# Causal attention on one core: row-score jobs in two PSUM banks, column-score jobs in four

## The reference, cut to what matters

```
dot  = einsum('bqhd,bkhd->bhqk', q, k)              # q, k scaled
dot  = where(tril, dot, -inf)
attn = softmax(dot, axis=-1)
out  = einsum('bhqk,bkhd->bqhd', attn, v) @ Wo
```

## Time and profile before

| | us |
|---|---|
| median of three timed runs | 4139.68 (4137.76 to 4142.01) |
| the profiled execution's own time | 4147.65 |
| its span in the profile | 4145.7 |
| PE busy in the span | 3816.1 |
| DVE busy | 2304.2 |
| ACT busy | 1747.5 |

### The profile page before, as it was taken

How to read it: one execution, slowest core, us unless ns; L and a number is a source line. 1 busy time by engine, 2 the same in 40 slices (tenths; PEclk the granted TensorE clock), 3 DMA queues, 4 the chain that set the end, 5 groups by cost and what they waited for, 6 DMA issues and landing times.

```text
span 4145.7 us, 77057 instructions
## 1 busy us (share of the span) xinstructions
PE 3816.1 (92%) x30311; PEld 2466.6 (59%) x30431; DVE 2304.2 (56%) x7434; ACT 1747.5 (42%) x3560; POOL 813.5 (20%) x1373
## 2 busy tenths in 40 slices
PE   7999999988899999998899989999889998999988
PEld 3555567665455556766545546676654555666665
DVE  4545444677454545467654554546765454454776
ACT  3324333466332433346633242335663334233566
POOL 3102013321110202332011020233302102023330
PEclk9999999999999999999999999999999999999999
DMA  2000000000000000000000000000000000000000
GB/s 81 1 1 1 1 1 1 2 2 1 12 1 1 1 1 1 1 2 2 5 8 1 1 1 1 1 1 2 2 6 7 1 1 1 1 1 1 2 2 6
DMA packets 19694, 17.06 MB, mean 4 GB/s; under 512 B 2604, under 2 KB 18941, under 8 KB 19325
## 3 DMA queue, kind: packets, MB, share of 16 engines
q1 hardware_dynamic: 19325, 11.99, 1.0%
HBM read 9.89 MB, written 2.10 MB: 3 GB/s over the span
## 4 chain that ended last, share of the span: by engine, by line
PE 70%; DVE 11%; ACT 8%; POOL 7%; issue 4%; DVEq 0%; POOLq 0%; SPq 0%
PE banks L1033 8%; PE banks L1047 8%; PE banks L1043 8%; PE banks L926 6%; PE banks L958 5%; POOL work L507 4%; PE banks L970 3%; PE banks L911 3%; PE banks L1142 3%; PE banks L1277 2%; ACT work L783 2%; PE banks L831 2%; ACT work L777 2%; PE banks L1114 2%; PE banks L1087 2%
## 5 line engine op out<-in xcount | busy, mean ns | idle before, releaser
L1454 DVE CUSTOM_DVE_ANT_0 work<-banks,mask_row 128x512 f32<-128x512 f32 (+3 forms) x1024 | 444.2, 487 | 248.3 <-PE banks L926 246.3
L669 ACT ACTIVATE work<-banks 128x384 f32<-128x384 f32 (+1 forms) x768 | 357.6, 532 | 373.9 <-PE banks L958 372.2
L687 ACT ACTIVATE work<-banks 128x512 f32<-128x512 f32 (+1 forms) x384 | 227.7, 596 | 650.7 <-PE banks L1043 641.8
L926 PE MATMUL banks<-work 32*128 32x512 f32 (+3 forms) x2048 | 421.5, 460 | 13.0 <-ACT work L662 13.0
L958 PE MATMUL banks<-work 32*128 32x512 f32 (+3 forms) x2048 | 425.8, 464 | 4.3 <-DVE work L1463 4.3
L474 POOL TENSOR_SCALAR_AFFINE_SELECT work<-work 128x128 f32<-128x128 f32 (+1 forms) x768 | 250.1, 332 | 878.8 <-ACT work L669 860.5
L1531 DVE TENSOR_TENSOR work<-work,banks 128x512 f32<-128x512 f32 (+1 forms) x384 | 261.1, 686 | 280.2 <-PE banks L1047 280.2
L464 POOL TENSOR_TENSOR rstd<-rstd,half 128x4 f32<-128x4 f32 x64 | 64.6, 1009 | 1755.2 <-DVE rstd L1388 1755.2
L1033 PEld LDWEIGHTS banks<-wd,work 128*128 128x128 f32 (+1 forms) x3072 | 359.3, 191 | 49.1 <-issue 49.1
L1033 PE MATMUL banks<-wd,work 128*128 128x128 f32 (+1 forms) x3072 | 361.1, 274 | 0.0
L926 PEld LDWEIGHTS banks<-work 32*128 32x128 f32 x2048 | 232.4, 183 | 167.1 <-DVE work L1454 93.6
(11 more groups left out here) (312 smaller groups left out, 6723.0 us busy)
## 6 DMA issues: line engine op xcount, KB each, us to landing
wg<-in_L_ffn_Wg_dram SPq DMA_DIRECT2D x1, 1376.0 KB
wu<-in_L_ffn_Wu_dram SPq DMA_DIRECT2D x1, 1376.0 KB
x_a<-in_L_attn_a_x_dram SPq DMA_DIRECT2D x4, 256.0 KB, 2.8
x_b<-in_L_attn_a_x_dram SPq DMA_DIRECT2D x4, 256.0 KB, 2.9
wd<-in_L_ffn_Wd_dram SPq DMA_DIRECT2D x2, 512.0 KB
out_dram<-x_a SPq DMA_DIRECT2D x4, 256.0 KB, 2.3
out_dram<-x_b SPq DMA_DIRECT2D x4, 256.0 KB, 2.5
wk_l<-in_L_attn_a_Wk_dram SPq DMA_DIRECT2D x1, 512.0 KB, 6.2
```

The lines of the kernel that those rows point to most:

```text
L669: eng.activation(prob4[:, G % 2, hh, C_AT[j]:C_AT[j] + C_N[j]], bank(column_bank(c))[:, 0:C_N[j]], ACT.Exp).then_inc(s_exp, 1)
L926: m = eng.matmul(bank(k % 3)[:, col:col + N], q4[own, G, P * t:P * t + P], k4[own, G, 0:N], start=True, stop=True)
L1454: m = eng.tensor_tensor_reduce(out=summed[:, k % 2, col:col + N], in0=bank(k % 3)[:, col:col + N], in1=mask_row[:, T - N:T], scale=1.0, sc ...
```

## The change

Row jobs turn in two banks (0 and 1) in place of three, so row job k waits for the maximum of job k - 2. Column jobs up to 32 turn in four banks (2 to 5) in place of three and wait for the exponential of the job four before. From job 33 on the five banks come in the order 1, 3, 4, 5, 2, and only job 33 still waits for all row maxima; job 34 waits for an exponential as the later ones do.

```diff
         def column_bank(c):
-            return 3 + c % 3 if c < WIDE else 1 + (c - WIDE) % 5
+            return 2 + c % 4 if c < WIDE else (1, 3, 4, 5, 2)[(c - WIDE) % 5]
...
             def score_rows(k):
...
-                if k >= 3:
-                    eng.wait_ge(s_max, JOBS4 * n + k - 2)
+                if k >= 2:
+                    eng.wait_ge(s_max, JOBS4 * n + k - 1)
...
-                    m = eng.matmul(bank(k % 3)[:, col:col + N], q4[own, G, P * t:P * t + P], k4[own, G, 0:N],
+                    m = eng.matmul(bank(k % 2)[:, col:col + N], q4[own, G, P * t:P * t + P], k4[own, G, 0:N],
...
             def score_columns(c):
...
-                if WIDE <= c < WIDE + 2:
+                if c == WIDE:
                     eng.wait_ge(s_max, JOBS4 * (n + 1))
-                elif c >= WIDE + 2:
+                elif c > WIDE:
                     eng.wait_ge(s_exp, JOBS4 * n + c - 4)
-                elif c >= 3:
-                    eng.wait_ge(s_exp, JOBS4 * n + c - 2)
+                elif c >= 4:
+                    eng.wait_ge(s_exp, JOBS4 * n + c - 3)
...
                 def row_max(k):
...
-                        m = eng.tensor_tensor_reduce(out=summed[:, k % 2, col:col + N], in0=bank(k % 3)[:, col:col + N],
+                        m = eng.tensor_tensor_reduce(out=summed[:, k % 2, col:col + N], in0=bank(k % 2)[:, col:col + N],
```

## The result

The changed kernel takes 4573.11 us (median of four runs, 4562.64 to 4575.5) against 4140.62 us before: a ratio of 1.1044, 95% interval 1.1026 to 1.1063. It is slower by 432 us, 209 more than forecast, and above the upper end of the range, 4440.

The account below looks back on a forecast made before the run. PE, busy 92% and 70% of the chain, was taken as the bound, with row jobs waiting for the vector engine. Bank turns summed to 13.96 us a call, times 16 = 223 us, giving 4363 us; range 4250 to 4440.

Parts of the forecast that it names:

- the early part: From a call's first row job to the values, four bursts of three row jobs: +6.73 us a call.
- the middle part: From the values to the first column job: +0.62 us a call.
- the joint part: From the first column job to the weighing behind row job 47: +1.83, +1.26, +0.50, +0.48 twice, +1.03 twice, us a call.
- points 3 to 6: Jobs 16 to 23 +1.83; 24 to 26 +1.26, 36 to 38 +0.50; two fours +0.48 each; two fives +1.03 each.
- Points 1 and 3 to 6: First: projecting part's four bursts, third job waits for the first, +1.92, +1.61, +1.56, +1.64 us; the others: job groups from 16 on.
- Point 7: Fourth bank of the column jobs: gains at most 1.7 us a call, at least nothing; taken as nothing.
- the third rival: PE's granted clock falls to half through the projecting part: 159 us on top, 4522 us; 8%.
- The joint part hides nothing: Answers the rival that from k = 16 on existing waits hide the new ones: only 118 us, 4257 us; 12%.
- The not-slower case: PE's own stream is the bound, and the fourth column bank gives back 26.8 us: 4113 us; 5%.
- the signs that I named: Row waits doubled, 200 to 300 us; column waits near nothing; bursts 2.4 to 3.0 us; first column job 7.4 later; clock 1.00.

Follow-up runs that it names:

- the kernel with the fill before row job 14: Changed kernel plus idle products before each early burst's third job and one before row job 14, none in the joint part; 4444.22 us.
- the moved third job: Changed kernel with the third row job of each early burst put behind the next projection, the last burst's behind the values; 4433.9 us.

## Why the prediction was wrong, and what of it was right

**The sum was right, its clock was not.** At full clock the early part grew by 16.30 - 9.53 = 6.77 us (forecast 6.73), the middle part by 5.51 - 4.92 = 0.59 (0.62), the joint part by 34.52 - 27.92 = 6.60 (points 3 to 6: 1.83 + 1.26 + 0.50 + 0.96 + 2.06 = 6.61). That is 13.96 us a call, 223 us in all, and the kernel that fills the stops comes to 4378 us. Points 1 and 3 to 6 hold one by one too. The bursts of an early part at full clock without idle products (call 10 of the kernel with two banks there alone) grew by 2.00, 1.58, 1.55 and 1.63 us (forecast 1.92, 1.61, 1.56 and 1.64); points 3 to 6 measure 1.84, then 1.25 and 0.49, 0.48 and 0.47, 1.03 and 1.03 in call 1 of the kernel with the fill before row job 14. So this is not a sum of errors that cancel. Point 7 stands in its number: the columns' part is worth nothing.

**The step that failed is a term that the sum put at nothing, the clock.** Every product and turn in it is taken at full clock. I let the third rival stand at 8%, confined it to the early part (159 us on top), and set the range's upper end without it, because "in each 4.6 us of the new projecting part PE stands for some 0.8 only". The clock fell in all 16 calls, in the joint part of each. Added up over the calls, the early parts are 317.3 us long where 16 at full clock make 260.8, 56 us more; the middle ones 110.5 for 88.2, 22 more; the joint ones 692.9 for 552.3, 141 more. Of these 219 us, the joint part that I left out holds two thirds. The price of the rival in the early part alone, 159 us, was in turn too high: the clock comes back within the part.

The three parts together grew by 164.9 + 31.8 + 246.2 = 443 us, while the span grew by 415.0 (4145.7 to 4560.7). The 28 us between them were gained outside these parts. Of these, 26 lie between the last weighing of a call and the first projection of the next, 8 of them in the eight stretches where the next attention call follows at once. All eight had a mean clock of 0.54 to 0.72 before; five of them have 1.00 in the changed kernel. In front of call 3, before and after:

```profile
358.35:365.02 6.67, 5.06 (x29) 0.59 0.00 0
435.74:440.60 4.86, 3.21 (x30) 1.00 0.00 0
```

In this pair of profiles, then, the low clock costs 219 us within the three parts, beside 223 us of turns, and 28 us are gained elsewhere. Why the clock stood higher between the calls is not shown.

**Why my evidence misled me.** I argued from PE's busy share: 0.39 us busy of two did not bring the clock down, so stops of 0.8 us would not the earlier trace rows. In the changed kernel the recorded busy share does not tell a stretch before a fall from others. Two windows, before and after the fall at the start of call 0's joint part:

```profile
60.00:63.20 3.20, 3.20 (x12) 1.00 0.00 0
63.20:66.20 3.00, 3.00 (x11) 0.50 0.00 0
```

PE is recorded as busy throughout in the 3.2 us before the clock falls, whereas the 0.39 us busy of two in the earlier trace rows were followed by ten more microseconds at 1.00. What in PE's work decides it is not shown. A record counts a row job on one strip as busy like a product on the whole array, but the idle products that held the clock are products on one strip too, and no run varies this. The kernel before held a sign that the prediction did not use: it already issues products whose results nothing reads, at line 980 behind row jobs 12 and 13 and at line 831 ahead of the output projection.

The Trainium skill's passage that I set beside the rival ("TensorE: Matmul & The Clock Gate", A second HAM failure mode: psum-queue depth-cycling) describes a clock that oscillates when PE stops briefly again and again while it turns through PSUM banks; the traces here agree: in call 1 of the changed kernel the clock falls three times and comes back each time, and the mean clock is 0.63 to 0.83 in the joint parts of the changed kernel and 0.91 to 1.00 once the stops are filled.

**The other rivals.** The joint part hides nothing: with two banks there alone the kernel loses 121 us (4261.2 against 4140.63 in the same comparison). My text for this rival counted nine stops for row maxima from k = 16 on; nine is the number of the whole call, and five of them lie there (jobs 18, 27, 30, 39 and 42). The not-slower case has nothing for it. Of the signs that I named, the doubled number of waits, the bursts (2.4 to 3.1 us where the clock holds) and the unchanged part with columns alone came. The first column job of call 0 came 10.6 us later after the first row job in place of 7.4, which it has at full clock. The column jobs' waits did not go, since 32 of them lie where columns run alone, and the clock of 1.00 did not come.

## What to carry to other kernels

A buffer less costs a whole turn (product, signal, read, signal) at each place where a list in program order reaches it early, and at full clock this could be summed here from a few rows to a per cent; the wait costs nothing where other work stands between, as the moved third job shows, though a job that is moved away from its neighbours then takes its own time. But where PE begins to stop often, work the sum at both levels of its clock and let the range hold the upper one: here the clock doubled the bill, 223 us of turns and some 209 more on balance. Whether an idle stretch of PE costs more than itself is quickly tried by filling it with products that nothing reads; that also gave the only kernel faster than the original, by 0.66%.

## What the runs showed of the hardware that was not expected

The granted clock fell to 0.50 at 63.20 us of the changed kernel's profile behind 3.20 us that the records show as fully busy. The same instructions held a clock of 1.00 in some calls and fell in others of the same execution: joint parts of 34.52 and of 47.44 us stand side by side in one profile of the kernel with fills before row job 14. More work on PE made the changed kernel 195 us faster.
